# Last stage of a two-layer gated block: products added one step later on VectorE, projected rows scaled ahead of the power on GpSimd

## The reference

```python
# attention's output projection (int8 fake-quantized o and wp), gated into x
out = _qdq(o) @ _qdq(wp).T + bp
x = x + jnp.tanh(g_xattn[1]) * out
# last layer, on the layernorm of that x
xn = x_ln * rms * gamma
a_scale = 127.0 / (jnp.max(jnp.abs(xn), axis=-1, keepdims=True) + _EPS)
x_q = jnp.clip(jnp.round(xn * a_scale), -128.0, 127.0) / a_scale
x = x + jnp.tanh(g_ffn[1]) * (x_q @ w_q.T)       # w_q has the values -1, 0, 1 times a scale
```

## Time and profile before

| | before |
|---|---|
| median of three executions | 973.28 us |
| the profiled execution | 971.6 us |
| its span in the profile | 969.9 us |
| TensorE busy | 819.0 us (84%) |
| VectorE busy | 775.5 us (80%) |
| ScalarE busy | 566.8 us (58%) |
| GpSimd busy | 485.8 us (50%) |
| mean granted TensorE clock | 0.938 of full speed |

### The profile page before, as it was taken

The page is one execution under the profiler, slowest core; times in us unless marked ns, Lnnn a source line. Parts: engine busy times, 40 slices in busy tenths (PEclk is TensorE's granted clock), DMA queues, the critical chain, the costliest instruction groups (busy, mean ns, idle before and its releaser), DMA issues.

```text
span 969.9 us, 14895 instructions
## 1 busy us (share of the span) xinstructions
PE 819.0 (84%) x4375; PEld 355.8 (37%) x4375; DVE 775.5 (80%) x1544; ACT 566.8 (58%) x959; POOL 485.8 (50%) x560
## 2 busy tenths in 40 slices
PE   1279989778999999999999978699989898985654
PEld 1245445333444444454444433132222222222221
DVE  3959999887899989999999758477788888846784
ACT  2348888754446656566566554466666666674562
POOL 1186556322343444334344343476675757676661
PEclk9859999999999999999999995899999999997795
DMA  8637887652323232332323332222223222000111
GB/s 277 221 95 191 216 232 199 159 147 44 66 55 75 57 64 55 59 60 54 65 54 62 60 80 72 83 60 62 71 57 87 62 81 68 8 13 5 44 66 65
DMA packets 171692, 86.09 MB, mean 89 GB/s; under 512 B 123488, under 2 KB 156400, under 8 KB 171632
## 3 DMA queue, kind: packets, MB, share of 16 engines
q1 hardware_dynamic: 171632, 85.38, 34.5%
HBM read 37.50 MB, written 12.58 MB: 52 GB/s over the span
## 4 chain that ended last, share of the span: by engine, by line
PE 54%; DVE 9%; issue 4%; SPq 4%; ACT 3%; DMA 3%; POOL 0%; DVEq 0%; ACTq 0%
PE bank L1091 22%; PE bank L1103 10%; PE bank L1149 4%; PE bank L1178 4%; PE bank L1168 4%; DMA A<-B 3%; PE bank L1286 3%; SPq L437 2%; PE bank L1187 2%; PE bank L1197 2%; DVE B L1631 1%; PE bank L1121 1%; SPq L446 1%; DVE B L1639 1%; PE bank L1157 1%
## 5 line engine op out<-in xcount | busy, mean ns | idle before, releaser
L1091 PE MATMUL bank<-A,B 128*128 128x512 f16 x1024 | 233.9, 382 | 3.8 <-DVE B L1548 3.8
L1631 DVE TENSOR_REDUCE B<-bank 128x1 f32<-128x512 f32 x256 | 167.3, 681 | 61.5 <-PE bank L1149 60.8
L915 ACT ACTIVATE A<-bank 128x512 f32<-128x512 f32 x256 | 143.9, 593 | 106.6 <-PE bank L1168 104.6
L577 POOL TENSOR_TENSOR B<-B 128x512 f16<-128x512 f32 x64 | 75.5, 1179 | 208.5 <-ACT B L799 154.1
L1091 PEld LDWEIGHTS bank<-A,B 128*128 128x128 f16 x1024 | 100.6, 99 | 127.4 <-DVE B L1548 4.6
L651 POOL TENSOR_TENSOR B<-A 128x512 f32<-128x512 f32 x64 | 81.0, 1297 | 99.9 <-ACT A L915 99.9
L1103 PE MATMUL bank<-A,B 128*128 128x512 f16 x512 | 120.6, 379 | 0.0
L1168 PE MATMUL bank<-A 98*128 98x512 f16 x256 | 94.0, 388 | 22.5 <-ACT A L915 11.4
L794 ACT ACTIVATE bank<-B 128x512 f32<-128x512 f32 x64 | 38.5, 602 | 125.4 <-DVE B L1542 125.2
L1149 PE MATMUL bank<-A 96*128 96x512 f16 x256 | 98.6, 412 | 7.2 <-DMA A<-B 4.1
L651 POOL TENSOR_TENSOR B<-B,A 128x512 f32<-128x512 f32 x64 | 79.1, 1265 | 0.5 <-ACT A L915 0.5
(11 more groups left out here) (233 smaller groups left out, 1488.4 us busy)
## 6 DMA issues: line engine op xcount, KB each, us to landing
B<-in_L_ffn_w_dram SPq DMA_DIRECT2D x48, 256.0 KB, 3.8
A<-k_parts SPq DMA_DIRECT2D x48, 128.0 KB, 2.7
A<-B SPq DMA_DIRECT2D x192, 32.0 KB, 1.9
X<-in_x_dram SPq DMA_DIRECT2D x4, 1024.0 KB, 13.6
B<-in_ctx_dram SPq DMA_DIRECT2D x16, 256.0 KB, 4.8
k_parts<-B SPq DMA_DIRECT2D x16, 256.0 KB, 4.4
v_rows<-B SPq DMA_DIRECT2D x16, 256.0 KB, 2.8
B<-v_rows SPq DMA_DIRECT2D x16, 256.0 KB, 3.2
```

Of the source, the lines that this page charges most:

```text
L577: nc.gpsimd.tensor_tensor(HLb[j][:, 1, :], Db[j % 2], HLb[j][:, 0, :], ALU.subtract).then_inc(lo_done, 1)
L915: nc.scalar.activation(PR[(HG * t + j) % 8], bank[2 + j % 2][:, :], ACT.Exp, scale=SCALE).then_inc(exp_done, 1)
L1091: last = mm(bank[2 * n + q][:, :], XQT[a][:, m, :], wt[:, m % DB, j * 512:j * 512 + 512], start=(m == 0), stop=(m == 2 * DB - 1))
L1631: reduce(NMX[g % 2][:, t, j:j + 1], bank[ROW_BANKS[r % 3]][:, :], AX.X, ALU.max, negate=True).then_inc(row_max, 1)
```

## The change

VectorE's `z_add` moves from the end of step s for unit s-3 to the place behind `z_ints` in step s for unit s-4, so the last one falls into a step of its own (s = 11). `ZSC` gets two buffers, since a unit's scale is now still wanted when the next one's is written. On GpSimd the product with `swp_all` of unit s-1 now stands ahead of the power of unit s-2, and the one-element add on `held` is gone. TensorE's, ScalarE's and SyncE's lists are as before.

```diff
-        FV, FR, ZM, ZAM, ZR, ZSC = (sc3[:, n, 0:2] for n in range(6))
+        FV, FR, ZM, ZAM, ZR = (sc3[:, n, 0:2] for n in range(5))
+        ZSC = [sc3[:, n, 0:2] for n in (5, 6)]
...
             def out_step(s, live):
-                if live(s - 2):
-                    pool.wait_ge(st4, s - 1)
-                    nc.gpsimd.tensor_tensor(FR, FV, half[:, 0:2], ALU.pow).then_inc(f_ready, 1)
                 if live(s - 1):
                     u = s - 1
                     pool.wait_ge(ro_ready, u + 1)
                     on_both = lambda v: v[:, :].rearrange("p (a d) -> p a d", a=1).to_broadcast([P, 2, D])
                     nc.gpsimd.tensor_tensor(RO, RO, on_both(swp_all), ALU.mult).then_inc(ro_scaled, 1)
+                if live(s - 2):
+                    pool.wait_ge(st4, s - 1)
+                    nc.gpsimd.tensor_tensor(FR, FV, half[:, 0:2], ALU.pow).then_inc(f_ready, 1)
+                if live(s - 1):
                     pool.wait_ge(ro_scaled, u + 1)
-                    nc.gpsimd.tensor_tensor(held[:, 0:1], held[:, 1:2], held[:, 1:2], ALU.add)
                     rows = X[:, bass.ds(u * 2, 2), :]
                     nc.gpsimd.tensor_tensor(rows, rows, RO, ALU.add).then_inc(x3_ready, 1)
...
-                    last_ = stt(row(u, t), bank[2 + t][:, :], ZSC[:, t:t + 1], row(u, t), ALU.mult, ALU.add)
+                    last_ = stt(row(u, t), bank[2 + t][:, :], ZSC[u % 2][:, t:t + 1], row(u, t), ALU.mult, ALU.add)
...
                 if live(s - 3):
                     z_ints(s - 3)
+                if live(s - 4):
+                    z_add(s - 4)
                 if live(s) and 2 * s >= AHEAD:
                     o_ints(s)
                 if live(s - 2):
                     z_scales(s - 2)
-                if live(s - 3):
-                    z_add(s - 3)
                 if live(s - 2):
-                    up_to(dve, z_added, s - 2)
-                    link(ts(ZSC, ZAM, LSC, None, ALU.mult))
+                    up_to(dve, z_added, s - 3)
+                    link(ts(ZSC[s % 2], ZAM, LSC, None, ALU.mult))
 
-            for s in range(UNITS + LAG):
+            for s in range(UNITS + LAG + 1):
                 out_step(s, lambda u: 0 <= u < UNITS)
```

## The result

The median of 20 executions is 976.46 us; 20 executions of the kernel before have 974.04 us. The ratio is 1.0025, 95% interval 1.0014 to 1.0037: 2.4 us slower, where 1.9 us were forecast. This lies inside what was called the same. The absolute time is 1.3 us above the forecast of 975.2 us; 0.8 us of that is the kernel before, whose median is 974.04 us over 20 executions and was 973.28 over three.

A forecast was written before the change was run, and what follows sets the result against it. VectorE's list plus its waits bounds the last stage; about 6 us of old TensorE waits is nearly all spent on waiting for `f_ready`. Sum +1.9 us, forecast median 975.2 us, range 969.5 to 981.5.

The forecast's parts named there:

- what was called the same: Whole kernel: a time from 968.4 to 978.2 us, about 0.5% (4.9 us) either way; chance 0.64.
- The loop through ScalarE and GpSimd: Last stage, step length: from Z (end of L1755, `zs_ready`) to the next 9.22 us, GpSimd's product standing before its power.
- The wait for it: VectorE ahead of `z_scales`: waits about 1.6 us for GpSimd's power (`f_ready`) in each of steps 3 to 8.
- The port, in step 2: VectorE's L1740 meets GpSimd's product on the shared port and is blocked, near 1.9 us; 0.9 us between the two outcomes.
- The walk: Step-by-step count through the last stage: Z(2) at 894.7, Z(8) at 951.6, end at 968.5 against 966.64.
- The port, in steps 6 and 7: VectorE's `o_ints`, issued at Z+4.1 behind `z_add`, is blocked by GpSimd's product until Z+5.0; the step is 9.7 us.
- TensorE: Projections late for ScalarE: at most 0.35 us, step 4 alone; steps 6 and 7 make the next step 0.15 us late.
- rival B: Slower: TensorE sets the pace, both projections at low clock, 1.4 us late six times: 8.4 us, 983.6 us; chance 0.12.
- my own case: Whole kernel within about 3 us of 975.2 us, chance 0.67; sign: steps 3 to 5 and 8 last 9.2 to 9.6 us.
- The tail: Step 9 to the end: last `z_ints` starts 6.95 us after the last `st4`, then 7.83 us to the end.
- Rival A: Slower: GpSimd's product gets the ports ahead of `z_ints`, 1.2 us in each of six steps, 7.4 us, 982.6 us; chance 0.13.
- Rival C: Faster: GpSimd's product is over before the power is wanted, 1.4 us six times, 8.5 us, 966.7 us; chance 0.08.

The follow-up runs named there:

- the change with `WPT` first: The whole change, with TensorE's `WPT` projection for step s put ahead of its `WLT` projection; 973.82 us, ratio 0.9999 to the kernel before.
- the late wait: The whole change, with VectorE waiting for `f_ready` only ahead of the first operation that reads FR; 970.21 us, ratio 0.9967 to the kernel before.
- two ahead: The whole change, with two added VectorE maximum operations, results unread, between `st4` and `z_ints`; 983.40 us, ratio 1.0097 to the kernel before.

## Why the prediction was right

**The loop through ScalarE and GpSimd.** Forecast: the next Z after 9.22 us. The kernel after had 9.13 us from Z(2) at 896.98 to Z(3) at 906.11, and the change with `WPT` first repeated 9.13 us in step after step. The terms hold one by one: from Z to the end of the copies 2.52 us, the product 2.35, the power 0.71, `z_scales` 3.49.

**The wait for it.** Forecast: about 1.6 us in each of steps 3 to 8. Measured at L1748: 3.11, 2.46, 2.65, 0.60, 0.60 and 2.23 us. The sum is near (11.6 us for 9.6), the single waits aren't: where `z_add` is there, `o_ints` isn't, and TensorE is in time, the wait is near 1.6 us (1.78, 1.78 and 1.76 us in steps 4, 5 and 8 of the change with `WPT` first). Step 3 has no `z_add` in front (1.4 us more), `o_ints` fills steps 6 and 7, and TensorE's lateness adds in the others. The loop sets the pace either way.

**The port, in step 2.** Forecast: L1740 blocked, near 1.9 us. The timeline of the kernel after:

```profile
889.68 2.35 POOL L665 TENSOR_TENSOR B<-B,swp_all 128x1024 f32<-128x1024 f32 x1 [1.44 <-ACT B L946]
...
890.27 1.78 DVE L1741 TENSOR_SCALAR B<-mv 128x2 f32<-128x2 f32 x1
```

It took 1.78 us and ended with the product. The dearer end was the right one to take, and L1782 the right row to take it from. The walk set the end of L1740 0.17 us behind the product's, while its own rows had held operations end 0.02 us behind the earlier trace rows; so Z(2) came 13.50 us after the start of the stage, for a forecast of 13.68 us. That it would be held at all was a choice between two ends 0.9 us apart, not something the rows had shown.

**The port, in steps 6 and 7.** Forecast: `o_ints` held from Z+4.1 until the product ends, step 9.7 us. Measured: `o_ints` (L1728) took 1.71 and 1.97 us, the power 1.15 us, and the distances from Z to Z were 9.58 and 9.84 us.

**TensorE.** This term was too small. I gave it 0.35 us in step 4 and 0.15 us each for what steps 6 and 7 hand on to steps 7 and 8, 0.65 us in all. ScalarE's waits at L946 for TensorE were 0.57, 0.76, 0.15 and 0.35 us for steps 4, 5, 7 and 8, 1.83 us. The rows of step 3 that I called the worst weren't: in step 4 the second projection took 3.13 us, not 2.70, with a granted clock of 0.60 of full speed in that stretch, where it had been 0.70 in rows 6.

```profile
911.50 3.59 PE L1287 MATMUL bank<-WLT,B 128*128 128x512 f16 x8 [2.15 <-ACT B L960]
...
914.88 3.13 PE L1287 MATMUL bank<-WPT,B 128*128 128x512 f16 x8
```

The second omission is that a delay is handed on: the late L946 puts off L955 and L960 behind it, so this `WLT` projection started at Z+5.39 and not at Z+4.72, and step 5, to which I gave nothing, waited most. So a part of rival B came true, about 1.2 us more than my term. Its sign, L946 waiting for TensorE in most steps, was there in four of the six, though at a fifth of its price; and the sign given for my own case, 9.2 to 9.6 us in steps 3 to 5 and 8, failed in steps 4 and 5 (9.82 and 10.00 us).

**The tail.** Forecast: the last `z_ints` 6.95 us after the last `st4`, 7.83 us from there to the end. The timeline of the kernel after:

```profile
956.72 0.17 DVE L1741 TENSOR_SCALAR B<-mv 128x2 f32<-128x2 f32 x1
...
963.66 0.69 DVE L1762 TENSOR_SCALAR B<-B 128x1024 f16<-128x1024 f32 x1 [1.32 <-issue]
...
970.19 1.41 DVE L1767 SCALAR_TENSOR_TENSOR X<-bank,B,X 128x512 f32<-128x512 f32 x2 [4.51 <-PE bank L1287]
```

963.66 − 956.89 = 6.77 us, and 971.60 − 963.66 = 7.94 us.

**The sum.** From Z(2) to Z(8) I had 56.9 us; the kernel after took 954.95 − 896.98 = 57.97. This and small terms of either sign make 2.50 us in the stage in place of 1.9.

**Rival A** did not come about: in every step from 3 to 8 `z_ints` started ahead of the product, by 0.7 us where TensorE was in time (898.83 and 899.57 in step 3) and by 1.0 to 1.6 us where it was late (907.97 and 909.39 in step 4). The runs also show that I described it badly. I took a margin of 0.6 us after which the whole 1.2 us is lost in each of six steps. When `z_ints` comes only just first it is the product that loses, 0.4 us; and when the order does turn, TensorE's delay in that step turns it back in the next. So its price is not six times one step's: with two ahead the order turned in two of the six steps.

**Rival C** did not come about either: with nothing to delay the power the step took 7.96 us, near the 7.8 us given for it, but that needed GpSimd's old order (or the late wait, steps from 7.7 us).

## What to carry to other kernels

When an operation is brought forward on one engine because its input is early, write down who reads what now stands behind it: here a power over two numbers was put behind 2.35 us of work, and a full-size stage of another engine hung on it. A wait belongs in front of the first instruction that reads the value, not at the top of the block: moving this one behind 2.5 us of independent work was worth 6 us. And change parts one at a time: one part here was worth −4.5 us and the other +12.2, and the pair came out at +2.4.

## What I had not expected of the hardware

A VectorE tensor_scalar with two numbers in a partition was held for a whole GpSimd instruction, 2.32 us for 0.17, even with its source strided, while operations with one number in a partition (L1752 at 911.98 in the kernel with the late wait, in the middle of GpSimd's add) run at their usual 0.33 us for two. A reciprocal of two numbers wasn't held either (L1753 of the kernel before, 0.17 us at 892.50, beside the add of 891.47). That GpSimd's product loses when it starts 0.14 us later, and then only about the rest of the other's instruction (0.4 us more, with 0.54 us of `z_ints` left by the records), fits the rule in the Trainium skill (SBUF — State Buffer, Who interferes with whom) that issue order decides and that the second one blocks until the first is done. These runs agree with it in both directions.

The time ahead of the stage, which no kernel of the study touches, varies by several us between profiled executions: the first product started at 881.02 us before, between 881.07 and 884.96 in ten of the experiments, and at 878.58 in the eleventh. A difference of spans between two profiles would have given 4.9 us where the change made 2.4.
